# Keys from hi and lo parts, copies of x behind the second weight piece, and reordered waits

## The reference

```
qkv = x @ w_qkv.T ; q, k, v split in 16 heads of 16
L   = q k^T / 4 ;  L_y = q (x @ w_ky.T)^T / 4
agg = sum_k( exp(clip(L_y, -15, 15)) * causal ) + 1e-6
r   = log(|L| + 1e-6) - log(agg + 1e-6)
w   = softplus(r) * causal ;  A = w / (sum(w) + 1e-6)
x   = layernorm(x + (A v) @ w_proj.T)
h   = silu(x W1 s1) * (x W2 s2) ; h = gelu(h H1 t1) ; h = gelu(h H2 t2)
out = layernorm(x + h W3 s3)          # W1, W2: 256 to 1024, H1, H2: 1024 to 1024, W3: 1024 to 256
```

## Time and profile before

| | |
|---|---|
| runs | 1240.26 us median of 3 (1237.6 to 1240.6) |
| the profiled execution | 1239.5 us |
| its span, first to last instruction | 1237.8 us |
| TensorE busy | 1184.8 us (96%), granted clock 0.988 of full over the span |
| VectorE, ScalarE, GpSimd busy | 714.9 us (58%), 659.0 us (53%), 205.5 us (17%) |
| DMA | 117.28 MB, mean 95 GB/s |
| chain that ended last | 80% TensorE, 9% VectorE, 5% issue, 4% ScalarE |

### The profile page before, as it was taken

The page is one execution under the profiler, slowest core; times in us unless marked ns, Lnnn a source line. Parts: engine busy times, 40 slices in busy tenths (PEclk is TensorE's granted clock), DMA queues, the critical chain, the costliest instruction groups (busy, mean ns, idle before and its releaser), DMA issues.

```text
span 1237.8 us, 23984 instructions
## 1 busy us (share of the span) xinstructions
PE 1184.8 (96%) x8222; PEld 805.6 (65%) x8222; DVE 714.9 (58%) x1178; ACT 659.0 (53%) x1004; POOL 205.5 (17%) x238
## 2 busy tenths in 40 slices
PE   6899999999999999879999999999999999999997
PEld 2444444544444444437888888888888888888886
DVE  3577778787878787875345435344344353443444
ACT  4688989899888888755114133232242332322421
POOL 2434333434333333300000000000000000000000
PEclk7999999999999999989999999999999999999999
DMA  5555758576776765277000100001000001000010
GB/s 150 120 141 136 215 158 223 156 228 166 216 191 186 204 169 144 56 234 268 34 34 1 36 16 17 34 0 34 17 0 34 17 17 34 0 34 17 0 34 18
DMA packets 62544, 117.28 MB, mean 95 GB/s; under 512 B 8992, under 2 KB 14624, under 8 KB 62496
## 3 DMA queue, kind: packets, MB, share of 16 engines
q1 hardware_dynamic: 62064, 116.12, 32.9%
q10 hardware_dynamic: 432, 0.52, 0.2%
HBM read 46.35 MB, written 19.92 MB: 54 GB/s over the span
## 4 chain that ended last, share of the span: by engine, by line
PE 80%; DVE 9%; issue 5%; ACT 4%; DMA 1%; DVEq 0%; POOL 0%; ACTq 0%; POOLq 0%; SPq 0%
PE score_banks L1360 53%; PE acc_bank L1272 8%; PE score_banks L1244 6%; DVE w_ring L904 4%; PE misc_bank L1236 3%; PE misc_bank L1199 3%; PE misc_bank L1340 2%; ACT w_ring L656 2%; ACT e_ring L649 1%; PE misc_bank L1303 1%; DVE base_v L957 1%; DVE e_ring L895 1%; PE misc_bank L1207 1%; PE misc_bank L1319 1%; DVE e_ring L889 1%
## 5 line engine op out<-in xcount | busy, mean ns | idle before, releaser
L728 ACT ACTIVATE f_h_full<-score_banks,f_scales 128x512 f32<-128x512 f32 x128 | 87.5, 689 | 340.8 <-PE score_banks L1360 340.7
L904 DVE TENSOR_TENSOR w_ring<-score_banks,keep 128x1024 int32<-128x1024 int32 (+1 forms) x192 | 194.0, 1040 | 28.1 <-PE score_banks L1244 27.3
L1360 PE MATMUL score_banks<-f_ha_hi,f_w_all 128*128 128x512 f32 x512 | 204.0, 399 | 0.0
L1360 PE MATMUL score_banks<-f_hb_hi,f_w_all 128*128 128x512 f32 x512 | 203.6, 398 | 0.0
L1360 PE MATMUL score_banks<-f_hb_lo,f_w_all 128*128 128x512 f32 x512 | 201.6, 394 | 0.0
L1360 PE MATMUL score_banks<-f_ha_lo,f_w_all 128*128 128x512 f32 x512 | 200.8, 392 | 0.0
L656 ACT ACTIVATE w_ring<-w_ring 128x1024 f32<-128x1024 f32 (+1 forms) x192 | 172.5, 918 | 24.3 <-DVE w_ring L904 24.2
L649 ACT ACTIVATE e_ring<-score_banks 128x1024 f32<-128x1024 f32 (+1 forms) x192 | 158.3, 877 | 39.4 <-PE score_banks L1244 36.0
L513 POOL TENSOR_SCALAR_AFFINE_SELECT e_ring<-e_ring 128x512 f32<-128x512 f32 (+1 forms) x96 | 80.4, 837 | 285.8 <-DVE e_ring L895 145.0
L1082 DVE CAST f_ha_hi<-f_h_full 128x512 fp32r<-128x512 f32 x64 | 27.3, 426 | 160.5 <-ACT f_h_full L728 160.5
L1360 PEld LDWEIGHTS score_banks<-f_ha_hi,f_w_all 128*128 128x128 f32 x512 | 96.1, 188 | 24.6
(11 more groups left out here) (143 smaller groups left out, 1759.1 us busy)
## 6 DMA issues: line engine op xcount, KB each, us to landing
piece<-in_wf SPq DMA_DIRECT2D x44, 256.0 KB, 2.9
wf_copy<-piece SPq DMA_DIRECT2D x44, 256.0 KB, 3.0
ky_stack<-ky_hi SPq DMA_DIRECT2D x64, 128.0 KB, 2.4
ky_stack<-ky_lo SPq DMA_DIRECT2D x64, 128.0 KB, 2.4
k_stack<-k_hi SPq DMA_DIRECT2D x64, 128.0 KB, 2.6
k_stack<-k_lo SPq DMA_DIRECT2D x64, 128.0 KB, 2.6
f_w_all<-wf_copy SPq DMA_DIRECT2D x2, 4096.0 KB, 24.6
f_x_turn<-x SPq DMA_DIRECT2D x9, 512.0 KB, 3.2
```

The source lines that it names most:

```text
L728: nc.scalar.activation(h_full[m % 2][:], f_bank[m % F_RING], ACT.Gelu, scale=scales[:, 1 + layer, m:m + 1]).then_inc(gelu_done, 1)
L904: nc.vector.tensor_tensor(w_ring[:, t % RING, 2 * i:2 * i + 2, 0:cols].bitcast(I32), pair_banks(place(t, i), cols).bitcast(I32), keep[:, a ...
L1360: mm = nc.tensor.matmul(out, left.bitcast(dt), right.bitcast(dt), start=first and n == 0, stop=last and n == 1)
```

## The change

K is projected from hi and lo parts: the weights of the third kind are split too (`split_weights(2)`), `k_proj` runs six fp32r matmuls on `xk_hi` and `xk_lo`, and these are copies of `xq_hi` and `xq_lo`, made by two DMAs of 512 KB per batch (`copy_x`) from SBUF to SBUF. In half 0 SP issues them behind the second piece, in front of `stack_qc`. `split_x` waits for them. `xv` is still loaded, for v.

The rest: `e_ring` has three buffers instead of two; the last check of a slot moves from beat 4 to the end of beat 5; `add_differences` moves from the end of beat 1 to its start; in the beats 1 and 2 VectorE takes the first pair's mask before the clip (`FIRST_PAIR`); the second `turn` and its copy move behind the beat's last sums; five dummy matmuls run after the first projections (`STACK_WARM`); in `beginning` the scores of beats 3 and 4 go ahead of the projections of ky and q; the lists of `ending` are written in a new order, with `project_out(b, 1)`, its `residual` and the last weight sum moved into the first feed-forward chunk.

```
-E_RING = 2
+E_RING = 3
+STACK_WARM = 5
-CHECK_BEATS = (0, 2, 3, 4)
+CHECK_BEATS = (0, 2, 3, 5)
+FIRST_PAIR = (1, 2)
-        END_ZONE, Y_ZONE, SHARED = 23 * 1024, 80 * 1024, 185 * 1024 - 128
+        END_ZONE, Y_ZONE, SHARED = 23 * 1024, 102 * 1024, 185 * 1024 - 128
...
# SP
+            def copy_x(b):
+                reach_alone(sp, k_ready, 2 * b, sp_passed)
+                reach_alone(sp, xq_split, b + 1, sp_passed)
+                for there, here in ((xk_hi, xq_hi), (xk_lo, xq_lo)):
+                    sp.dma_start(there[:].bitcast(F32), here[:].bitcast(F32)).then_inc(xk_in, 16)
...
                 if check and check != "last":
                     load_piece(k, 1, check)
+                if k.half == 0:
+                    copy_x(k.batch)
                 if 3 in w:
                     stack_qc(k.shift(-1), 0)
...
# ScalarE
             def split_x(b):
                 reach(act, q_ready, 2 * b)
+                reach(act, xk_in, 32 * b)
...
                     if t == 5 and k.half == 1:
                         v_keep(k)
+                    if t == 5 and check_step(t, check) is not None:
+                        check_piece(k, check_step(t, check))
...
                     if t == CHUNKS:
                         copy_sums(k, 0, (True, 0 in w))
+                    if t == 3 and output is not None:
+                        turn_keep(output, 1)
...
# ScalarE, ending: the lines that move
                 keep_att(u, 1, True)
+                base_make(u)
                 logs(k, 0, 1)
+                v_sum_keep(u)
                 logs(k, 1, 0)
...
+                logs(k, 4, 0)
                 turn_keep(b, 0)
                 logs(k, 4, 1)
                 logs(k, 5, 0)
+                turn_keep(b, 1)
                 logs(k, 5, 1)
...
# VectorE, slot
+                    if t == 1 and check_step(0, check) is not None:
+                        add_differences(k.index - FIRST_CHECK - 1)
                     if t == 1 and before[0]:
                         keep_agg(k.shift(-1), 1)
                         factors(k.shift(-1))
...
+                    elif t in w and t in FIRST_PAIR:
+                        absolute(k, t, (0,))
+                        clip(k, t)
+                        absolute(k, t, (1,))
...
# VectorE, ending
+                absolute(k, 0, (0,), w_pair_alone)
                 keep_agg(u, 1)
                 factors(u)
+                absolute(k, 0, (1,), w_pair_alone)
                 qc_make(u)
+                absolute(k, 1, (0, 1), w_pair_alone)
                 absolute(k, 2, (0, 1), w_pair_alone)
+                absolute(k, 3, (0, 1), w_pair_alone)
+                absolute(k, 4, (0, 1), w_pair_alone)
+                sum_differences()
                 divide_sums(b)
+                absolute(k, 5, (0, 1), w_pair_alone)
...
# TensorE
             def k_proj(u):
                 take_misc((k_made, u.index + 1))
-                reach(pe, xv_in, 16 * (u.batch + 1))
-                project_t(u, 2, xv, k_ready)
+                reach(pe, xk_in, 32 * (u.batch + 1))
+                project_split(u, 2, k_ready, x_hi=xk_hi, x_lo=xk_lo)
...
+                if (layer, m) == ("gated", 0):
+                    sum_weights(Unit(BATCH, 1), 2, True)
+                if (layer, m) == ("gated", 1):
+                    project_out(BATCH - 2, 1)
...
# TensorE, slot: behind sum_weights
+                    if t == 3 and output is not None:
+                        turn(output, 1)
...
# TensorE, beginning
                 sum_exps(k, 0, True)
+                scores_y(k, 3, y_pair_alone, 1)
                 ky_proj(k1)
-                scores_y(k, 3, y_pair_alone, 1)
                 sum_exps(k, 1, True)
+                scores_y(k, 4, y_pair_alone, 1)
                 q_proj(k1)
...
# TensorE, ending, new order
                 spread_c(u)
+                sum_values(u)
+                sum_prefixes(u)
                 sum_weights(k, 0, True)
                 scores_w(k, 2, False)
                 sum_differences()
+                scores_w(k, 3, False)
                 sum_weights(k, 1, True)
+                scores_w(k, 4, False)
+                sum_weights(k, 2, True)
+                flip_sums(k, 0, (False, True))
+                scores_w(k, 5, False)
+                sum_weights(k, 3, True)
+                scores_w(k2, 0, False)
                 turn(b, 0)
+                sum_weights(k, 4, True)
+                scores_w(k2, 1, False)
                 turn(b, 1)
+                sum_weights(k, 5, True)
+                flip_sums(k, 1, (False, True))
+                scores_w(k2, 2, False)
+                sum_weights(k2, 0, True)
                 project_out(b, 0)
...
             project_split(Unit(0, 0), 0, q_ready, range(DT), acc)
+            for _ in range(STACK_WARM):
+                nc.tensor.matmul(score[0:2, 2 * BANK_PAIRS - 1, :], ones[:], acc_copy[:], start=True, stop=True)
-            pe.wait_ge(kind_made[2], 2 * DT)
+            pe.wait_ge(w_lo_made, 3)
```

More of the change, by code:

```diff
@@ L764, in slot @@
                         logs(*beat_before(k, t), 1)
-                    if check_step(t, check) is not None:
+                    if t < 5 and check_step(t, check) is not None:
                         check_piece(k, check_step(t, check))
@@ L1076, in chunk @@
                         lo(c, m - 1, ha_hi, ha_lo)
+                    if done is None and m == 2:
+                        residual(BATCH - 2, 1)
                 lo(c, FT - 1, ha_hi, ha_lo)
@@ L1130, in slot @@
                         add_base(divide)
-                    if t == 1 and check_step(0, check) is not None:
-                        add_differences(k.index - FIRST_CHECK - 1)
             def beginning(k, k1):
@@ L1194, in take_misc, with project_split @@
                 misc_readers[:] = readers
-            def project_t(u, kind, x, done):
-                m = slice(P * u.half, P * u.half + P)
-                for kt in range(DT):
-                    mm = nc.tensor.matmul(misc[:], w_in[:, kt, kind, m], x[:, kt, :], start=kt == 0, stop=kt == DT - 1)
-                mm.then_inc(done, 1)
-            def project_split(u, kind, done, kts=range(DT), bank=misc):
+            def project_split(u, kind, done, kts=range(DT), bank=misc, x_hi=xq_hi, x_lo=xq_lo):
                 m = slice(P * u.half, P * u.half + P)
@@ L1469, in slot @@
                         ky_proj(k.shift(1))
-                    if t in (2, 3) and output is not None:
-                        turn(output, t - 2)
+                    if t == 2 and output is not None:
+                        turn(output, 0)
                     if t == 2 and norm is not None:
```

62 lines of the change are left out of this document (19 added, 43 removed).

## The result

The changed kernel takes 1253.23 us (median of 4 runs, 1252.09 to 1258.8) where the kernel before takes 1240.17 beside it: ratio 1.0116, 95% interval 1.0099 to 1.0133, so slower by 1.2%, clear of noise. The forecast was 1244 us and the upper end of the range 1252. The profiled execution takes 1253.85 us with a span of 1252.1, which is 14.3 more than before. Up to the last value projection of the attention part 8.1 us of these are lost, between there and the end of the first feed-forward gates 6.2, and behind that nothing.

The account below looks back on a forecast made before the run. TensorE was taken to bound the kernel, with ScalarE as near to the end in the attention loop. Terms -1.0, +5.0 and -0.5, the others 0, gave +3.5 on 1239.5: 1243.0, forecast 1244 us after the runs' median; range 1233 to 1252.

Parts of the forecast that it names:

- K: Projection from hi and lo parts: 0.32 us shorter each, about 0.1 us won in ten loop projections; -1.0 us, bounds -5.1 and 0.
- start: Before and after the first scores: dummy matmuls may keep the clock up; -0.5 us, bounds -2.8 and +1.7.
- I take 1.0 us: Loop, scores of beat 3 in half 0: TensorE's wait for the late qc_lo stack, middle of 0 and 1.9 us.
- So it isn't given back: Loop: work after the late stack is chained on ScalarE, so its wait stays lost; five batches, +5.0 us.
- about -1.0 in waits: Last beats of attention: two waits of 4.0 us in all attacked, three new ones appear; net about -1.0 us.
- about one log, 1.0 us: Last beats: logs of beats 4 and 5 and scores behind divide_sums each hold TensorE by 1.0 us.
- cost there what they cost here: project_out and the last weight sum, moved into the feed-forward part where TensorE is the bound, cost the same there.
- the half clock would eat what the waits gain: Last beats: a longer half clock eats about -1.0 us of waits; term 0, bounds -4.0 and +3.0.
- the wait goes over to flip: Second turn in the loop: TensorE's 0.69 us wait goes, but flip waits for ScalarE's copies instead; 0, bounds -3.5 and 0.
- the stacks two microseconds or more late: Rival: copies at load pace behind full backlog, 1.9 us in each of five batches, cold ending +2; 1251 us, chance 0.20.
- The copies drain in time: Rival: 1 MB moves in under 3.5 us, qc_lo lands before 280.6, the +5.0 goes; about 1236 us, chance 0.35.
- The 66.5 us that were to confirm the sum: Loop batch in the changed profile: 66.5 us would confirm the summed terms, under 65.5 refute them.

## Why the prediction was wrong

The mechanism that it let decide was right, two sizes were not, and one term that it set to zero had a sign. A chain of kernels gives the terms by ratios (1240 times the difference of two ratios, each known to some 3 us); the profiled runs give them by stretches:

| term | forecast | by ratios | by stretches of the profiled runs |
|---|---|---|---|
| first pair, second turn, check, e buffer | 0 | -3.5 | -2.5 in the loop (-0.6 in most even slots, 0 in odd ones) |
| K, with copies at the end of the odd slot | -1.0 | -3.1 | -1.1 in the loop (0 in odd slots) |
| copies, from there to the changed place | +5.0 (0 to 9.5) | +13.8 | +10.9 in the loop |
| start | -0.5 | -1.6, not told from nothing | +1.4 up to the first value projection |
| ending | 0 (-4.0 to +3.0) | +8.8 | +6.1 |
| sum | +3.5 | +14.4 | +14.3 between the two spans, the stretches left out here included |

**Copies: the failed step is "I take 1.0 us" and the bound of 9.5 that goes with it.** The landing was inside its bounds: 281.1 to 282.5 on the old clock is 6.6 to 8.0 us behind the store, measured 7.5; and the wait, forecast 0.5 to 1.9, is 1.27 to 2.01, 1.6 in the mean. "So it isn't given back" was right too: where the clock stays, the slot is 32.74 against the 31.36 of the kernel with the copies elsewhere, longer by the wait of 1.30 and hardly more. Two things failed. The wait is 1.6 us and not 1.0, 7.9 us in the loop in place of 5.0. And the price of a wait was taken to be its length: behind three of the five the clock fell, and the filled waits show 1.2 us a time to be the clock's. Over 31.36 us each, the five even slots are 11.9 us longer, of which 7.9 are the waits and nearly all the rest the clock's. Rows that warn of it were at hand: the half clock of the earlier trace rows follows a wait of 5.92 us, and that of the earlier trace rows sets in at 543.3 us, behind two waits close to each other, while behind the 2.38 us the clock stays at 1.00 for five us. The prediction let these rows speak for start and ending alone.

```profile
541.36 0.85 PE L1244 MATMUL score_banks<-qc_stack,k_stack 32*128 32x128 f32 x16 [0.45 <-DVE w_ring L904]
...
543.21 1.04 PE L1330 MATMUL misc_bank<-ident,base_v 128*128 128x128 f32 x4 [1.00 <-ACT att_t L676]
```

**Ending: the failed steps are "about -1.0 in waits" and, in it, the three new waits of "about one log, 1.0 us".** At like clock (0.92) the waits of the stretch grow by 2.2 us, from 8.7 to 10.9. Of the three, one came, longer (1.63); the other log's wait (1.20) was there before (1.18), and the scores behind divide_sums wait for nothing. The largest new wait, 2.01 us, wasn't seen: the flip takes the bank that VectorE's sum reads, and that sum stands on VectorE behind the masks of two more beats. The two pieces "cost there what they cost here": 2.1 us, but what they left was filled by waits. That the half clock would eat what the waits gain was right in kind and small in size: a mean of 0.81 in place of 0.92 is 2.5 to 3.7 us.

**First pair and second turn: "the wait goes over to flip" is true and still not a zero.** The flip waits 0.40 us for the turn's copy, the exp sum 0.36 for the mask; removed were 0.69 and 0.49. The difference, 0.42, is most of the 0.6 us that an even slot gains, less than what was removed and more than nothing.

**K** was right in its mechanism: six matmuls of 1.66 us, then a wait for the log, 0.17 us in half 0 and 0.25 in half 1. Odd slots win nothing; most even ones win 0.3 us, though only when no stack is late. By stretches its -1.1 us is the size that was forecast; the -3.1 by ratios is hardly clear of nothing.

**Start:** the clock rose from 0.50 to 0.62 in 18 to 26 us, as announced, and TensorE was busy 5.25 us there in place of 5.57. The totals can't tell the rest. The traces speak against a gain: the first value projection starts at 38.8 to 40.1 us in the six profiled runs with the new start, and at 37.1 to 39.8 us in the ten with the old one and the copies, 1.4 us earlier in the mean.

The rivals: the stacks two microseconds or more late with a cold ending on top, 1251 at a chance of 0.20, comes nearest, 2 us short, and in part by luck. It had the stack 1.9 us late in five batches and half that in batch 7; the waits are 1.6 us in the mean, and none in batch 7. The clock that fell in the loop, which it didn't have, made up for that. Its cold ending of 2 us is 6.1 us, only part of it by the clock. "The copies drain in time" failed by the landing. The 66.5 us that were to confirm the sum were passed: 67.2 in the mean of five batches. Errors of both signs made the total nearer than its parts: the loop's other edits and K gave back 3.5 us in the loop by stretches and 6.6 us in all by ratios, where the forecast had 1.0.

## What to carry to other kernels

A new wait of TensorE costs its length and, where the clock falls behind it, that as well: here 1.2 us a time on a wait of 1.5 to 2.0 us, and nothing behind other waits as long. Look in the trace of before for what follows waits, above all two close to each other, and price both outcomes. Before asking how long a transfer takes, read who stands behind it on its queue: the same megabyte cost 11 us in the loop ahead of one small stack, and next to nothing at the end of the odd slot. When a wait is moved by a new order, follow each bank to its last reader, and count work moved out of a waiting stretch at its full price.

## What the runs showed that was not expected

The same order of the last nine beats took 40.8 us in one kernel and 44.5 in another, with nearly the same waits; by the mean clocks 6.5 us of the one were at 0.50, and 16.9 us of the other. The old order took 38.07 us at 1.00 and 40.65 at 0.92 with the same waits. Where the granted clock falls is thus set neither by the order alone nor by the length of a wait: in the changed kernel waits of 1.51, 1.84 and 2.01 us inside a busy slot were followed by some 3 us at 0.50 and those of 1.27 and 1.30 us were not, but in two kernels near it waits of 2.08 and 2.54 us were not either. Matmuls on constants in a wait kept the clock at 1.00 in every slot of the loop and in all three filled endings. The Trainium skill ("TensorE: Matmul & The Clock Gate", Part 1) says that activity releases the throttle; these runs agree, and show that activity without any use does as well.
